# An adaLN attention and feed-forward layer on one core: first norm's shift and scale as columns, x in three buffers, a new order of the work

## What is computed

```python
mod = (silu(c) @ wmod).reshape(4, 6, 1, 256)          # c: 4 x 256, wmod: 256 x 1536
sa, ca, ga, sb, cb, gb = (mod[:, i] for i in range(6))
ga, gb = (sign(g) * max(abs(g), 0.25) for g in (ga, gb))
h = layernorm(x) * (1 + ca) + sa
x = x + ga * attention(h)       # 16 query heads, 4 key/value heads, d = 16, causal, rope
h = layernorm(x) * (1 + cb) + sb
x = x + gb * ffn(h)             # rmsnorm, router, v/o projection, rmsnorm, silu(gate) * up, down (704 wide)
```

## Time and profile before

| | us |
|---|---|
| median of 3 runs | 510.67 |
| lowest and highest of the 3 | 510.49, 515.2 |
| the profiled execution, its own time | 510.83 |
| its span, first to last instruction | 509.1 |

### The profile page before, as it was taken

The page is one execution under the profiler, slowest core; times in us unless marked ns, Lnnn a source line. Parts: engine busy times, 40 slices in busy tenths (PEclk is TensorE's granted clock), DMA queues, the critical chain, the costliest instruction groups (busy, mean ns, idle before and its releaser), DMA issues. The chain is left out here.

```text
span 509.1 us, 9484 instructions
## 1 busy us (share of the span) xinstructions
...
## 2 busy tenths in 40 slices
...
GB/s 226 256 27 1 22 3 42 1 48 0 2 23 1 3 42 1 2 88 2 23 52 2 3 43 1 1 47 23 85 0 8 8 1 43 1 1 42 1 1 84
DMA packets 18353, 16.07 MB, mean 32 GB/s; under 512 B 6265, under 2 KB 16958, under 8 KB 18306
## 3 DMA queue, kind: packets, MB, share of 16 engines
...
...
## 5 line engine op out<-in xcount | busy, mean ns | idle before, releaser
L761 PE MATMUL banks<-gTh,guhi 128*128 128x256 f32 x352 | 103.2, 293 | 1.7 <-DVE fft L1200 1.5
L862 ACT ACTIVATE PT<-banks 128x1024 f32<-128x1024 f32 (+3 forms) x96 | 75.3, 811 | 43.9 <-PE banks L678 38.5
L763 PE MATMUL banks<-gTh,gulo 128*128 128x256 f32 x352 | 99.1, 282 | 0.0
L762 PE MATMUL banks<-gTl,guhi 128*128 128x256 f32 x352 | 99.1, 282 | 0.0
L761 PEld LDWEIGHTS banks<-gTh,guhi 128*128 128x128 f32 x352 | 66.6, 189 | 6.3 <-issue 4.6
L762 PEld LDWEIGHTS banks<-gTl,guhi 128*128 128x128 f32 x352 | 66.7, 190 | 0.3
L763 PEld LDWEIGHTS banks<-gTh,gulo 128*128 128x128 f32 x352 | 66.7, 189 | 0.0
L1111 DVE TENSOR_REDUCE mxp<-banks 128x2 f32<-128x1024 f32 (+3 forms) x56 | 61.5, 1143 | 6.2 <-PE banks L657 3.0
L516 POOL TENSOR_SCALAR_AFFINE_SELECT PT<-PT 128x512 f32<-128x512 f32 x32 | 21.2, 662 | 66.0 <-ACT PT L862 65.9
L678 PE MATMUL banks<-QKT 128*128 128x512 f32 (+3 forms) x192 | 51.9, 369 | 2.3 <-ACT PT L862 1.3
L652 PE MATMUL banks<-QKT 128*128 128x512 f32 (+3 forms) x192 | 48.8, 364 | 5.8 <-ACT QKT L842 2.1
...
## 6 DMA issues: line engine op xcount, KB each, us to landing
...
QKT<-mrT SPq DMA_DIRECT2D x32, 4.0 KB
```

The source lines that it names most:

```text
L761: pe.matmul(out_, guhi[:, k, blk, :], gh, start=(m == 0 and k == 0), stop=False)
L762: pe.matmul(out_, guhi[:, k, blk, :], gl, start=False, stop=False)
L763: i = pe.matmul(out_, gulo[:, k, blk, :], gh, start=False, stop=(m == len(blocks) - 1 and k == KB - 1))
L862: act.activation(PT[:, u % 2, 2 * q:2 * q + 2, 0:CH - q0], both("prob", b, n)[:, :, 0:CH - q0], ACT.Exp, scale=float(D) ** -0.5).then_inc( ...
```

## The change

Six things are altered.

1. The first norm's shift and scale. A new PE step `pmodc` multiplies the first 512 columns of wmod, as the stationary side, by silu(c) (4 columns), so that the result lies with channels over partitions, for all 4 batches at once: 4 x 2 matmuls of 4 columns. A new DVE step `vmodc` copies it into `modc` (now 2 x 2 x 4 columns). `ldA` and its DMAs are gone, `wts` and `bias` read column b. `pmod` keeps the other 1024 columns (2 x 2 matmuls instead of 3 x 2), `vmod` copies two banks instead of three, `mod_dram` has 4 rows.
2. The first loads: wmod's first 512 columns (512 KB) go ahead of x, the other 1024 (1 MB) behind the rope tables. The first ACT instruction waits for c alone, `pmodc` for the first part, `pmod` for the rest.
3. x has three buffers `xres`, in which the batch is read, changed and stored; `xbuf` and `x1` are gone. `ldx` of batch 1 waits for nothing, that of batch 2 for `gwd` (the staged w_down lies in buffer 2), that of batch 3 for the store of batch 0. `x1`'s waits for the store and for the weights are gone.
4. `stats` waits for the previous batch's `rstd1`, and `rstd1` for its `norm1`, since several batches may now be under way.
5. `pprep0` waits for `vmodc`, as both use bank 3.
6. The whole `ORDER` is another one.

```diff
-V_CSL, V_SETW, V_MOD, V_FWVT = 2, 3, 8, 9
+V_CSL, V_SETW, V_MODC, V_MOD, V_FWVT = 2, 3, 4, 9, 10
+NX = 3
...
-SP_STEPS = dict(ldx=NC, ldA=1, ldW=1, ldB=1, ldG=1, mrd=NC, store=NC)
-S_STEPS = dict(setw=1, vmod=1, vprep0=1, vprep1=1, pmod=1, pprep0=1, pprep1=1, aprep=PIECES, awd=1, gprep=PIECES, gwd=1)
+SP_STEPS = dict(ldx=NC, ldW=1, ldB=1, ldG=1, mrd=NC, store=NC)
+S_STEPS = dict(setw=1, vmodc=1, vmod=1, vprep0=1, vprep1=1, pmodc=1, pmod=1, pprep0=1, pprep1=1, aprep=PIECES, awd=1, gprep=PIECES, gwd=1)
 COUNT = PE_STEPS | ACT_STEPS | DVE_STEPS | POOL_STEPS | SP_STEPS
...
 ORDER = """
-ldx ldx pmod stats rstd1 norm1 norm1 xT4 setw vmod pprep0 vprep0 pprep1 stats norm1 norm1 xT3 aprep aprep aprep ldA
-wts xev qkv4 xev bias5 qkv3 aprep vprep1 gprep gprep rstd1 norm1 norm1 norm1 norm1 xT2 xT0 gprep ldB xev qkv2 xev
-biasq qkvb qkvb rope sthi qkv3 qkvb stlo stack0 awd ldW wob stk stack4 stk ldA wts qkvb rope max0 max2 mxr mxr bias6
-max4 max0 sthi stlo mxr biasq max2 max4 mxr stack6 stk stack0 stk mxr max6 max2 mxr mneg mtT4 mrow max0 mrd ldG ldG
-mxr mxr max4 max6 max2 mxr mxr mxr max0 max4 prob6 mxr mxr mxr max2 prob0 exp prob6 max4 exp exp max0 mxr mxr mxr
-prob2 max6 exp pmask pv4 prob2 exp max0 mxr pmask gprep mxr prob2 prob6 exp pmask pv exp prob2 max0 pv exp pmask pv
...
-hlo h2 h2T0 h2hi h2lo ms2 ms2 rs2 h2 route route h2 had ms2 ms2 a2 route sum a3 gate0 gate1 sil up2 hsel fft gate7 rs2
-fin sil ffhi h2 h2T2 route h2hi hsel h2lo h2 had fflo sum hsel sum ms2 ms2 up3 up6 fft sil up2 gate4 up3 h2T5 rs2 zad
-fin ffhi ffl hsel fft h2 h2 gate6 up7 gate1 h2hi ffhi h2lo fflo sil h2T0 up4 up5 sil h2hi fft ffhi fflo h2lo down0 sil
-fft sum fft ffhi ffl ffhi gate6 down0 up1 sil fft sum fin fflo gate0 gate4 sil gate0 ffhi fft sil up5 ffhi fflo gate6
-sil fft ffhi sil fflo ffl zad down4 down6 fft ffhi gate5 up7 up0 down1 fft sil ffhi ffl sum sum fin fflo fft sum ffhi
-fflo down4 sum store store fin down5 sum down4 sum fin store
+ldx ldx stats rstd1 setw pmodc vmodc wts bias4 biasq pmod norm1 norm1 xT4 xev pprep0 qkv4 norm1 stats rstd1 norm1
+norm1 xT5 xev qkv5 norm1 norm1 norm1 xT6 vmod vprep0 xev ldx ldG ldx ldW pprep1 qkvb qkvb rope xT3 stats qkv6 qkvb
+aprep rstd1 gprep aprep sthi xev stlo vprep1 aprep aprep awd qkv3 stack6 stack4 qkvb stats rope gprep gprep gprep
+rstd1 stk max6 wts mxr max2 stk max4 max0 mxr max6 sthi max2 mxr stlo stack4 mxr mxr mxr mneg stk max4 mxr max6 mxr
+max2 max0 max4 stack6 mxr max2 mxr stk max6 mxr mxr mxr mtT4 mrow max0 max2 max4 max6 mxr max0 mxr max2 mxr mxr mxr
+mxr gwd mrd ldx prob4 exp prob6 max0 prob4 exp prob2 norm1 norm1 norm1 pmask mxr mneg prob6 ldB exp exp pv0 exp mtT1
+mrow prob2 norm1 pmask exp pmask prob6 prob4 xT1 xev pv pv norm1 stats ldx bias1 biasq wob exp exp pmask xT4 norm1
+norm1 norm1 pv mrd prob6 ldG ycopy yT5 ytm exp prob0 prob2 ynT5 prob6 exp pv0 stats rstd1 rstd1 ynev exp exp wo5 x1
...
-        xbuf = sb("xbuf", [P, NT, C])
-        x1 = sb("x1", [P, 2, NT, C])
+        xres = sb("xres", [P, NX, NT, C])
         xn, hbuf, dl, hh = (sb(name, [P, TPC, C]) for name in ("xn", "hbuf", "dl", "hh"))
...
+                sp.dma_start(xres[:, b % NX, c * TPC:(c + 1) * TPC, :], x[bass.ds(b, 1), c * CH:(c + 1) * CH, :].rearrange(
+                    "o (t p) c -> p (o t) c", p=P)).then_inc(s_x[c][b % NX], 16)
 
             for k in range(KB):
-                sp.dma_start(cT[:, k, :], c_in[:, k * P:(k + 1) * P].rearrange("b p -> p b")).then_inc(l_mod, 16)
+                sp.dma_start(cT[:, k, :], c_in[:, k * P:(k + 1) * P].rearrange("b p -> p b")).then_inc(l_c, 16)
+            sp.dma_start(wm_st[:, :, 0:CH], wmod[:, 0:CH].rearrange("(k p) n -> p k n", p=P)).then_inc(l_modc, 16)
             load_x(0, 0)
-            sp.dma_start(wm_st[:], wmod.rearrange("(k p) n -> p k n", p=P)).then_inc(l_mod, 16)
             sp.dma_start(wq_st[:], Wq.rearrange("(k p) n -> p k n", p=P)).then_inc(l_qkv, 16)
             sp.dma_start(wk_st[:], Wk.rearrange("(k p) n -> p k n", p=P)).then_inc(l_qkv, 16)
             sp.dma_start(wv_st[:], Wv.rearrange("(k p) n -> p k n", p=P)).then_inc(l_qkv, 16)
@@ -375,6 +375,7 @@
             load_x(0, 1)
             sp.dma_start(cos_t[:], rope_cos).then_inc(l_small, 16)
             sp.dma_start(sin_t[:], rope_sin).then_inc(l_small, 16)
+            sp.dma_start(wm_st[:, :, CH:6 * C], wmod[:, CH:6 * C].rearrange("(k p) n -> p k n", p=P)).then_inc(l_mod, 16)
             sp.dma_start(Wo_raw[0:H * D, :], Wo).then_inc(l_small, 16)
             sp.dma_start(Wo_raw[H * D:H * D + 1, :], bo.unsqueeze(0)).then_inc(l_small, 16)
...
-                if kind == "ldA":
-                    if b > 0:
-                        wait("wts", 0)
-                        wait("biasq", 0)
-                    for v in range(2):
-                        sp.dma_start(modc[:, v, :], mod_dram[bass.ds(b, 1), v * C:(v + 1) * C].rearrange(
-                            "o (k p) -> p (o k)", p=P)).then_inc(s_modA, 16)
-                elif kind == "ldW":
...
-                    wait("x1", (n + 1) * NJ // NC - N["x1"])
+                    if b == NX - 1:
+                        sp.wait_ge(s_setG, weights_split)
+                    elif b >= NX:
+                        sp.wait_ge(s_out[n], 16 * (b - NX + 1))
                     load_x(b, n)
                 elif kind == "mrd":
                     wait("mrow", n + 1)
...
                     wait("stats", n + 1)
+                    earlier("norm1", (n + 1) * TPC)
                     ts = slice(n * TPC, (n + 1) * TPC)
                     then(pool.tensor_scalar(nmean[:, ts], mv1[:, ts, 0], -1.0, 0.0, ALU.mult, ALU.add))
                     rsqrt(rstd1[:, ts], mv1[:, ts, 1], eps_ln[:, ts], S["rstd1"])
...
 
-                if kind == "pmod":
+                if kind == "pmodc":
 
                     pe.wait_ge(s_setV, V_CSL)
-                    for m in range(3):
+                    pe.wait_ge(l_modc, 16)
+                    for m in range(2 * KB):
                         for k in range(KB):
-                            i = pe.matmul(bank(m)[0:B, :], csl[:, k, :], wm_st[:, k, m * CH:(m + 1) * CH],
+                            i = pe.matmul(bank(3)[:, m * B:(m + 1) * B], wm_st[:, k, m * P:(m + 1) * P], csl[:, k, :],
+                                          start=(m == 0 and k == 0), stop=(m == 2 * KB - 1 and k == KB - 1))
+                    i.then_inc(s_setP, 1)
+                elif kind == "pmod":
+
+                    pe.wait_ge(s_setV, V_CSL)
+                    pe.wait_ge(l_mod, 16)
+                    for m in range(2):
+                        for k in range(KB):
+                            i = pe.matmul(bank(m)[0:B, :], csl[:, k, :], wm_st[:, k, (m + 1) * CH:(m + 2) * CH],
                                           start=(k == 0), stop=(k == KB - 1))
                     i.then_inc(s_setP, 1)
                 elif kind == "pprep0":
 
                     pe.wait_ge(l_ffn, 96)
                     pe.wait_ge(s_const, 3)
+                    pe.wait_ge(s_setV, V_MODC)
                     for d in range(KB):
                         for k in range(KB):
                             i = pe.transpose(bank(3)[:, (d * KB + k) * P:(d * KB + k + 1) * P],
...
+            act.wait_ge(l_c, 32)
             act.activation(cth, cT, ACT.Tanh, scale=0.5).then_inc(s_setA, 1)
 
...
+                    o = bank(3)[:, 0:2 * KB * B].rearrange("p (v k b) -> p v k b", v=2, k=KB)
+                    dve.tensor_copy(modc[:, 0], o[:, 0])
+                    assert setup(dve.tensor_scalar(modc[:, 1], o[:, 1], 1.0, None, ALU.add)) == V_MODC
                 elif kind == "vmod":
 
-                    dve.wait_ge(s_setP, 1)
-                    for m in range(3):
+                    dve.wait_ge(s_setP, 2)
+                    for m in range(2):
                         i = dve.tensor_copy(modr[:, m * CH:(m + 1) * CH], bank(m)[0:B, :])
                     setup_then(i)
-                    rows = modr.rearrange("b (m v n) -> b m v n", m=2, v=3)
-                    dve.tensor_scalar(rows[:, :, 1, :], rows[:, :, 1, :], 1.0, None, ALU.add)
-
...
-                        dve.wait_ge(s_setV, V_SETW)
-                    dve.wait_ge(s_modA, b * 32 + 32)
+                        dve.wait_ge(s_setV, V_MODC)
                     earlier("qkv", NJ)
                     for k in range(KB):
-                        i = dve.tensor_scalar(Wq_b[:, k, :], Wqkv[:, k, :], modc[:, 1, k:k + 1], None, ALU.mult)
+                        i = dve.tensor_scalar(Wq_b[:, k, :], Wqkv[:, k, :], modc[:, 1, k, b:b + 1], None, ALU.mult)
                     i.then_inc(S["wts"], 1)
                 elif kind == "wob":
                     if b == 0:
...
-                    if b == 1 and n == 0:
-                        dve.wait_ge(s_setG, weights_split)
-                    if b > 1:
-                        dve.wait_ge(s_out[2 * n // TPC], 16 * (b - 1))
                     two = slice(2 * n, 2 * n + 2)
```

(16 more changed lines are left out.)

154 lines of the change are left out of this document (86 added, 68 removed).

## The result

The change is faster: 492.73 us (median of 4, 491.66 to 494.12) against 510.58 (median of 4). The ratio is 0.9626, with a 95% interval of 0.9561 to 0.9692. I had said 504.5, in a range of 498 to 513: the direction was right, the gain was nearly three times what I had summed up. The profiled execution took 493.6, with a span of 491.8.

A forecast was written before the change was run, and what follows sets the result against it. PE was taken as the bound from 150 us, with setup, DVE and gaps limiting earlier stages. Head -0.5, fill -6.6 and last batch +0.9 made -6.2 us: 504.5 us against the median, range 498 to 513.

The forecast's parts named there:

- Further on: Batches 1 to 3: x in three buffers frees their loads from x1; taken as 0 us, bounds -1 and +1.
- rival 3: Later batches: the new order brings the 5.83 us stack wait back for batches 2 and 3; slower, 516 us, chance 0.16.
- Net 0.5: Up to the first prob of chunk 1: 3.2 us sooner less 2.7 leaves a gain of 0.5 us.
- The pair at `mneg.0.1`: DVE instructions in the first maxima: short once gwd moves away, with a long rope or wts instruction beside gwd instead.
- Rival 1: Head: the first mxr starts 4.5 us sooner and the head start is kept; 500 us, chance 0.24.
- The fill: Attention of batch 0 up to the second batch's stack: moved-up PE work saves 6.6 of 7.2 us of waits.
- rival 2: From 110 to 150 us DVE is the bound, so the fill is given back; 511 us, chance 0.18.
- no wait above 2 us: Sign to look for: no PE wait above 2 us between 100 and 120 us.
- The last batch: h2T.3.2 comes 5.5 us of PE work behind a.3.5, its chain is about 6.4 us: a cost of +0.9 us.
- three marks of being wrong: First mxr after 46; a stack wait over 3 us in a later batch; PE idle behind 150 over 3 us from 13.6.

The follow-up runs named there:

- e6: Changed kernel with down.0.4 and down.0.5 moved from between pv.1.11 and ynT.1.1 to behind wo.1.3, their sums with them: 499.39 us.
- e4: Kernel before with one added wait: GpSimd's fin.0.1, and zad.1.1 behind it, start only when rope.2.0 is done: 507.74 us.
- the hybrids: Changed kernel's instructions with its order cut at 205 us: old order then new, 510.03 us; new order then old, 508.92 us.
- f2: Kernel before with GpSimd's ffl.2.3 moved from ahead of rstd2.3.2 to behind hmod.3.2: 511.21 us.
- e3: Kernel before with ytm.1.1 moved ahead of rope.2.0 on VectorE: 510.31 us.
- e2: Changed kernel and order, but all of wmod multiplied first and shift and scale columns read back through DRAM for all batches: 503.4 us.
- e10: Changed kernel with the seven gate and up steps between pv.0.11 and stack.1.0 moved behind stack.1.0, their followers with them: 502.01 us.

## Why the prediction was wrong, and where it was right

**The step that failed** is "Further on". I took 0 us (bounds -1 and +1) for `ldx` and nothing for the new order itself between 150 us and the last batch. The reason I gave against rival 3, "PE is 96% full there, so the old list shows that it can be avoided", was the thought behind it. Two things were wrong. 96% of 330 us leaves 13.6 us of idle time, more than twice my whole forecast, and an order that is remade can take it: 7.2 us went. And the busy share counts half-clock stretches as full: the one at 216 us (3.4 us long, so 1.7 lost) is gone, as is another at 445. The count of work puts 11.8 us of gain behind 150, of which idle time and clock together (7.2 and twice 1.7) are 10.6. The 6.6 at 205 to 230 are explained: e6 shows 5.6 of them to be cover, and e4 takes 2.9 away by keeping POOL off the rope on DVE's queue. The 3.5 behind 430 and the 2.3 ahead of it are placed by the count only; the hybrids show that most of them go with the new order's own steps there, and f2 tried one step for the former and moved the wait instead. Little of the 3.5 can be the clock: e3 and e4 have the old order there and the same two waits of 1.1 us, ran at 1.00 around 445, and still lose 5.0 from 430 to 470 where the kernel before loses 5.5. What stays open is which steps of the new order gain there.

**The head.** Net 0.5 came true (0.6), in part because two errors cancel: the first prob of chunk 1 came 2.0 us sooner and not 3.3, and the PE work that the old kernel had done more by then is 1.9 us by the standard costs and not 2.7. The stages were within 2 us: `setw` at 11.5 (10), first qkvb 26.1 (24.5), first mxr 44.25 (44), `mtT.0.1` 71.0 (69), first prob of chunk 1 at 75.8 (74.5). pprep1 took 2.9 us, the value for the upper clock; I had taken 4. The pair at `mneg.0.1` is at 0.25 us, free of `gwd`, as I said, and `gwd` struck `stlo.0.1` instead (1.59 us for 0.42) rather than rope or wts. But e2 shows that "net 0.5" is a poor name for it. Against the same order with e2's head, which is later than that of the kernel before, it is worth 8 to 11 us; with e2's head the new order gains 7 us and not 18. Rival 1, "the head start is kept: 500", had a first mxr 4.5 us sooner, which did not come.

**The fill** was 6.6 in my sum, from waits alone, and is 7.2 to 9.3 (e10), with the clock behind them; rival 2, that it is given back, is wrong. One detail of it came true: `ytm.0.1` stands behind rope.1.0, and PE waited 2.4 us for it at 112, against my "no wait above 2 us".

**The last batch**, +0.9, isn't seen: from 430 to 470 us, where `h2T.3.2` stands (460.4), the kernel after loses 2.0 us where the one before lost 5.5. **Rival 3** had the right mechanism with the wrong sign: passages between batches do set several us each, but the new order made them shorter, not longer.

Of the three marks of being wrong, "PE's idle time behind 150 differs by more than 3 us" was the one that came: 6.4 against 13.6. The last matmul, forecast near 497, came at 486.
